# Transposing half of the row tiles on VectorE, and making low parts on GpSimd, in a low-pass MLP kernel

## What is computed

```python
# x: (16, 64, 64, 768) f32; W1: (192, 768); W2: (768, 192)
xs = einsum('bhwc,dc->bhwd', x, W1) + b1
xs = gelu(xs, approximate=False)
xs = fft_low(xs)    # 2D FFT over h, w; keep a centred 32 x 32 square of frequencies; inverse FFT; real; abs
xs = einsum('bhwd,cd->bhwc', xs, W2) + b2
return x + xs
```

## Time and profile before

| | |
|---|---|
| median of 3 runs | 2502.86 us (2502.48 to 2505.04) |
| the profiled execution | 2502.31 us, of it 2500.5 us span |
| busy: PE / DVE / ACT / POOL | 98% / 80% / 51% / 14% |
| granted PE clock | 0.995 |
| DMA | 709 MB, 284 GB/s, queue of SP 80.0% of 16 engines |

### The profile page before, as it was taken

One profiled execution on the slowest core, in us unless ns is written; L12 is line 12 of the kernel. 1 busy time (PEld: TensorE's weight loads), 2 busy tenths in 40 slices (PEclk: granted clock), 3 DMA queues, 4 the chain that ended last, 5 costly groups with the idle time before them and its releaser, 6 DMA issues.

```text
span 2500.5 us, 49622 instructions
## 1 busy us (share of the span) xinstructions
PE 2451.7 (98%) x16736; PEld 2423.6 (97%) x16736; DVE 1998.7 (80%) x4123; ACT 1272.9 (51%) x3076; POOL 350.6 (14%) x628
## 2 busy tenths in 40 slices
PE   8999999999999999999999999999999999999977
PEld 7999999999999999999999999999999999999967
DVE  6688888888888888888888888888888888888855
ACT  4555555555555555555555555555555555555532
POOL 1211111111111111111111111111111111111100
PEclk9999999999999999999999999999999999999998
DMA  6688888888888888888888888888788788878775
GB/s 201 227 281 288 291 291 292 282 299 284 295 288 293 292 285 300 286 291 291 290 293 284 299 287 290 293 288 299 280 300 290 284 292 289 296 282 299 250 281 225
DMA packets 233453, 709.29 MB, mean 284 GB/s; under 512 B 18706, under 2 KB 85522, under 8 KB 233236
## 3 DMA queue, kind: packets, MB, share of 16 engines
q1 hardware_dynamic: 233236, 706.40, 80.0%
HBM read 454.67 MB, written 251.66 MB: 282 GB/s over the span
## 4 chain that ended last, share of the span: by engine, by line
PE 95%; DMA 3%; issue 1%; DVE 1%; ACT 0%; SPq 0%; DVEq 0%; ACTq 0%
PE ps L285 23%; PE ps L272 13%; PE ps L286 11%; PE ps L331 8%; PE ps L333 7%; PE ps L332 7%; PE ps L336 7%; PE ps L339 7%; PE ps L319 5%; DMA cols<-filtered_rows 2%; PE ps L321 2%; PE ps L295 2%; PE ps L296 2%; PE ps L297 2%; DMA filtered_rows<-filt 0%
## 5 line engine op out<-in xcount | busy, mean ns | idle before, releaser
L378 ACT ACTIVATE xt_hi<-ps 128x512 fp32r<-128x512 f32 x768 | 460.1, 599 | 1121.1 <-PE ps L272 1119.0
L285 PE MATMUL ps<-w1s,xt_hi 128*128 128x384 f32 x3072 | 981.9, 375 | 0.0
L286 PE MATMUL ps<-w1s,xt_lo 128*128 128x192 f32 x3072 | 771.5, 251 | 0.0
L466 DVE TENSOR_TENSOR xt_lo<-ps,xt_hi 128x512 fp32r<-128x512 f32 x768 | 529.8, 690 | 288.3 <-ACT xt_hi L378 273.5
L518 DVE TENSOR_TENSOR xc<-ps,xc 128x384 f32<-128x384 f32 x1024 | 569.3, 556 | 135.3 <-PE ps L339 109.8
L286 PEld LDWEIGHTS ps<-w1s,xt_lo 128*128 128x128 f32 x3072 | 587.9, 191 | 0.0
L285 PEld LDWEIGHTS ps<-w1s,xt_hi 128*128 128x128 f32 x3072 | 578.9, 188 | 0.0
L272 PE MATMUL ps<-ident,xa 128*128 128x128 f32 x3072 | 462.0, 273 | 8.4 <-DMA xa<-x_dram 5.9
L272 PEld LDWEIGHTS ps<-ident,xa 128*128 128x128 f32 x3072 | 375.6, 141 | 25.5 <-issue 5.9
L331 PE MATMUL ps<-w2a_hi,oa_hi 128*128 128x384 f32 x1024 | 363.2, 355 | 0.5 <-DVE xc L518 0.5
L333 PE MATMUL ps<-w2b_lo,ob 128*128 128x384 f32 x1024 | 349.7, 341 | 0.0
(11 more groups left out here) (50 smaller groups left out, 2702.6 us busy)
## 6 DMA issues: line engine op xcount, KB each, us to landing
xa<-x_dram SPq DMA_DIRECT2D x256, 768.0 KB, 4.6
xc<-x_dram SPq DMA_DIRECT2D x256, 768.0 KB, 6.7
out_dram<-xc SPq DMA_DIRECT2D x256, 768.0 KB, 5.0
filtered_rows<-filt SPq DMA_DIRECT2D x256, 192.0 KB, 2.1
cols<-filtered_rows SPq DMA_DIRECT2D x128, 384.0 KB, 7.2
xc<-w1t_dram SPq DMA_DIRECT2D x1, 576.0 KB, 5.9
xc<-w2t_dram SPq DMA_DIRECT2D x1, 384.0 KB
xc<-w2t_dram SPq DMA_DIRECT2D x2, 192.0 KB
```

The source lines that it names most:

```text
L285: nc.tensor.matmul(ps_h[t % 2][:, 0:2 * D], hi, w1s[:, k, :], start=k == 0, stop=False)
L286: ins = nc.tensor.matmul(ps_h[t % 2][:, D:2 * D], lo, w1s[:, k, 0:D], start=False, stop=k == KC - 1)
L378: nc.scalar.activation(xt_hi[:, n % XT_SLOTS, :], ps_xt[n % 2][:], ACT.Copy).then_inc(s_xhi, 1)
L466: nc.vector.tensor_tensor(xt_lo[:, n % XT_SLOTS, :], ps_xt[n % 2][:], xt_hi[:, n % XT_SLOTS, :].bitcast(F32), ALU.subtract).then_inc(s_xlo, 1)
```

## The change

1. `xa` is split into `xv` (first tile of a pair) and `xe` (second tile). `xv` is loaded by four transfers: quarter a of the channels goes to partitions 32a to 32a + 31, pixels 32g + r to partition 32a + r and piece g. A 32x32-block transpose of DVE (`transpose_tile`) then gives the tile with channels on the partitions, in another channel order, for which `w1v` is a second, reordered copy of W1. ACT makes its high part from SBUF (`vt_hi_tile`), POOL the low part (`vt_lo_tile`).
2. The second tile is still transposed by PE, in two units of three blocks.
3. `hid_lo_pair` and `split_lo_pair` move from DVE to POOL. `split_lo_pair` runs in the turn of `filter_h_pair`, so `OUT` and the store come one turn earlier; `filter_h_pair` stands ahead of `filter_w_pair` and `out_half` in slot 0.
4. `cols` of later chunks are read a turn earlier. POOL packs at the end of its turn, and its list is written out in line, not in a loop.

```diff
-OUT = FILTER_H + 2
+OUT = FILTER_H + 1
+    x_quads = x.rearrange("b h w c -> b (h w) c").rearrange("b (t g r) c -> b t r g c", g=QUADS, r=32)
 ...
+            def load_xv(m, q):
+                until(sp, s_vt, PAIRS, m, q - X_SLOTS + 1)
+                n = q % X_SLOTS
+                for a in range(QUADS):
+                    sp.dma_start(xv[32 * a:32 * (a + 1), n, :, :],
+                                 x_quads[m, 2 * q, :, :, QC * a:QC * (a + 1)]).then_inc(s_xv[n], 16)
+            def load_xe(m, q):
+                until(sp, s_t, 2 * PAIRS, m, 2 * (q - X_SLOTS + 1))
+                n = q % X_SLOTS
+                sp.dma_start(xe[:, n, :], x_rows[m, :, 2 * q + 1, :]).then_inc(s_xe[n], 16)
 ...
-                    if (at := stage(i, s, READ_COLS)) and at[1] % 2 == 0:
-                        read_cols(at[0], at[1] // 2)
+                    if (at := stage(i, s, READ_COLS)) and (at[1] == 0 or at[1] % 2 == 1 and at[1] < PAIRS - 1):
+                        read_cols(at[0], (at[1] + 1) // 2)
 ...
 # PE
+            def transpose_unit(m, q, e):
+                if e == 0:
+                    until(pe, s_xe[q % X_SLOTS], 16 * PAIRS // X_SLOTS, m, 16 * (q // X_SLOTS + 1))
+                until(pe, s_xlo, 2 * PAIRS, m, 2 * q + e - 1)
+                for b in range(UNIT):            # UNIT = 3
+                    k = UNIT * e + b
+                    ins = nc.tensor.transpose(ps_xt[e][:, b * P:(b + 1) * P], xe[:, q % X_SLOTS, k * P:(k + 1) * P], ident[:])
+                ins.then_inc(s_t, 1)
+            def mm1_slot(m, q, j):               # four of the twelve (t, k); t 0 first
+                ...
+                    if t == 0:
+                        if k == 0:
+                            until(pe, s_vlo, PAIRS, m, q + 1)
+                        hi, lo, w1s = vt_hi[...], vt_lo[...], w1v
+                    else:
+                        if b == 0:
+                            until(pe, s_xlo, 2 * PAIRS, m, 2 * q + e + 1)
+                        hi, lo, w1s = xt_hi[...], xt_lo[...], w1e
 ...
+                            if j == 0:
+                                transpose_unit(*at, 1)
+                            if j == 2 and (after := next_pair(*at)):
+                                transpose_unit(*after, 0)
+                            mm1_slot(*at, j)
+                        if j == 0 and (at := stage(i, s, FILTER_H)):
+                            filter_h_pair(*at)
                         if j == 1 and (at := stage(i, s, LATE)):
                             filter_w_pair(*at)
 ...
                             for u in OUT_HALVES[j]:
                                 out_half(*at, u)
-                        if j == 0 and (at := stage(i, s, FILTER_H)):
-                            filter_h_pair(*at)
 ...
 # ACT, order of a turn: xt_hi_unit(pair, 1), gelu_pair(pair before), vt_hi_tile(next pair),
 #   split_hi_pair, xt_hi_unit(next pair, 0), stage_filtered
+            def vt_hi_tile(m, q):
+                until(act, s_vt, PAIRS, m, q + 1)
+                until(act, s_m1, SLOTS * PAIRS, m, SLOTS * (q - 2) + 2)
+                nc.scalar.activation(vt_hi[:, q % 2, :], vt[:, q % 2, :], ACT.Copy).then_inc(s_vhi, 1)
 ...
 # DVE, order of a turn: transpose_tile(next pair), xt_lo_unit(pair, 1), add_half; y_pair, hid_sum and
 #   hid_pre, add_half; xt_lo_unit(next pair, 0), hid_sum and hid_pre, two add_half
+            def transpose_tile(m, q):
+                until(dve, s_xv[q % X_SLOTS], 64 * PAIRS // X_SLOTS, m, 64 * (q // X_SLOTS + 1))
+                until(dve, s_vlo, PAIRS, m, q - 1)
+                nc.vector.transpose(vt[:, q % 2, :],
+                                    xv[:, q % X_SLOTS, :, :].rearrange("p g (k c) -> p k g c", c=32)).then_inc(s_vt, 1)
 ...
 # POOL, order of a turn: hid_lo_pair, corner_pair, vt_lo_tile(next pair), split_lo_pair, pack_cols_b
+            def hid_lo_pair(m, q):
+                pool.wait_ge(s_gelu, PAIRS * m + q + 1)
+                until(pool, s_f, PAIRS, m, q - 1)
+                nc.gpsimd.tensor_tensor(hid_lo[:, q % 2, :, :], hid[:, q % 2, :, :], hid_hi[:, q % 2, :, :].bitcast(F32),
+                                        ALU.subtract).then_inc(s_hlo, 1)
+            def vt_lo_tile(m, q):
+                until(pool, s_vhi, PAIRS, m, q + 1)
+                nc.gpsimd.tensor_tensor(vt_lo[:, q % 2, :], vt[:, q % 2, :], vt_hi[:, q % 2, :].bitcast(F32),
+                                        ALU.subtract).then_inc(s_vlo, 1)
+            def split_lo_pair(m, r):
+                until(pool, s_hi, PAIRS, m, r + 1)
+                yr, hi, o = y_abs[:, r % 2, :, :], oa_hi[:, r % O_SLOTS, :, :], ob[:, r % O_SLOTS, :, :]
+                nc.gpsimd.tensor_tensor(oa_lo[:, r % O_SLOTS, :, :], yr[:, 0:2, :], hi.bitcast(F32), ALU.subtract).then_inc(s_alo, 1)
+                pool.wait_ge(s_alo, PAIRS * m + r + 1)
+                nc.gpsimd.tensor_tensor(o[DB:P, 0, :], yr[0:DB, 2, :], o[0:DB, 0, :].bitcast(F32), ALU.subtract).then_inc(s_blo0, 1)
+                pool.wait_ge(s_blo0, PAIRS * m + r + 1)
+                nc.gpsimd.tensor_tensor(o[0:DB, 1, :], yr[DB:P, 2, :], o[DB:P, 1, :].bitcast(F32), ALU.subtract).then_inc(s_blo, 1)
+                pool.wait_ge(s_blo, PAIRS * m + r + 1)
```

More of the change, by code:

```diff
@@ L154, in until, with next_pair @@
                 eng.wait_ge(s, per_image * m + n)
+        def next_pair(m, q):
+            if q + 1 < PAIRS:
+                return m, q + 1
+            if whole(m) and m + 1 >= IMAGES:
+                return None
+            return m + 1, 0
         def turns(eng, turn):
@@ L523, in turn @@
                 for s in range(count):
-                    for j in range(UPP):
-                        if whole(i) and i == 0 and s == 0 and j == 0:
-                            for n in range(AHEAD):
-                                xt_lo_unit(0, n)
-                        if at := stage(i, s, 0):
-                            xt_lo_unit(at[0], UPP * at[1] + j + AHEAD)
-                        if j == 0 and (at := stage(i, s, SPLIT_LO)):
-                            split_lo_pair(*at)
-                        if j == 0 and (at := stage(i, s, LATE)):
-                            hid_lo_pair(*at)
+                    after = next_pair(*at) if (at := stage(i, s, 0)) else None
+                    for j in range(SLOTS):
+                        if i == 0 and s == 0 and j == 0:
+                            transpose_tile(0, 0)
+                            set_up_w1(w1v, w1vf, s_w1v_loaded, 64, s_w1v)
+                            xt_lo_unit(0, 0, 0)
+                            set_up_w1(w1e, w1ef, s_w1e_loaded, 16, s_w1e)
+                        if j == 0 and after:
+                            transpose_tile(*after)
+                        if j == 0 and (at := stage(i, s, 0)):
+                            xt_lo_unit(*at, 1)
+                        if j == 1 and (at := stage(i, s, FILTER_H)):
+                            y_pair(*at)
+                        if j == 2 and after:
+                            xt_lo_unit(*after, 0)
                         if j >= 1 and (at := stage(i, s, 0)):
@@ L540, in turn @@
                             corner_copy(at[0])
-                        if j == 1 and (at := stage(i, s, FILTER_H)):
-                            y_pair(*at)
                         if at := stage(i, s, OUT):
@@ L577, in turn @@
                 for s in range(count):
-                    packs = None
-                    if (at := stage(i, s, READ_COLS)) and at[1] % 2 == 0:
-                        packs = at[0], at[1] // 2
-                    if at := stage(i, s, LATE):
-                        corner_pair(*at, packs)
-                    elif packs:
-                        wait_to_pack(*packs)
-                    if packs:
-                        pack_cols_b(*packs)
-            turns(pool, turn)
+                    if i == 0 and s == 0:
+                        vt_lo_tile(0, 0)
+                    if at := stage(i, s, LATE):
+                        hid_lo_pair(*at)
+                        corner_pair(*at)
+                    if (at := stage(i, s, 0)) and (after := next_pair(*at)):
+                        vt_lo_tile(*after)
+                    if at := stage(i, s, FILTER_H):
+                        split_lo_pair(*at)
+                    if (at := stage(i, s, READ_COLS)) and at[1] % 2 == 0:
+                        pack_cols_b(at[0], at[1] // 2)
+            turns_in_line(turn)
 OUT_HALVES = [(0,), (1,), (2, 3)]
```

198 lines of the change are left out of this document (87 added, 111 removed).

## The result

The changed kernel takes 2419.4 us (median; 2412.8 to 2429.7), the kernel before 2504.0 (2502.5 to 2506.9): ratio 0.967, interval 0.9654 to 0.9685. It is faster by 84 us, where 138 were forecast; the time lies in the range, 54 us over the forecast of 2365. The profiled execution took 2429.7 us, its span is 2427.9; it is the slowest of the four, 10 us over their median, so the losses read from it are at their upper end.

A forecast was written before the change was run, and what follows sets the result against it. TensorE (PE), busy 98%, was taken as the bound, with DMA next. From 2502.3 us, 153 less for PE, +15 boundaries, +2 start, +5 image 0 and -6 tail gave 2365; 8-in-10 range 2340 to 2445 us.

The forecast's parts named there:

- PE, removed: Six of twelve transposes leave PE each turn (row pair): 0.64 us less, 9.47 to 8.83; 153 us over 239 turns.
- DVE and ACT: Per turn, DVE falls from 7.8 to 5.75 us, at most 6.7; ACT stays at 5.0; both under 8.83.
- POOL: POOL's low-part subtractions bring it to 6.1 to 7.2 us of an 8.83 us turn, leaning to 7.2: nearly full.
- Rival (c): POOL's turn passes 9.47 us if new columns cost 4.5 ns each; at 5 ns, 2700 us; chance 0.04.
- Rival (b): POOL or the wait chain comes late: `hid_lo` misses `filter_w_pair`, turn 9.0 to 9.2 us, about 2410; chance 0.12.
- none of these waits reaches PE: In the turn's layout, POOL's results come before PE asks, with about 0.9 to 2 us of slack.
- DMA: Quarter loads raise the tile from 1.03 to 1.4 to 2.15 us, the turn's DMA work to 8.1 to 8.9: just fits.
- rival (a): Transfers by quarters of the partitions become the bound: turn 9.2 us, about 2440 us in all; chance 0.18.
- Image boundary: PE stalls for `cols` of the next image by 1.0 us, range 0 to 3, at 15 images: +15 us.
- Start and image 0: A second W1 copy at the start costs +2 us; image 0 costs +5 instead of a gain of 10.
- Tail: Tail turns of about 6.4 us for 6.6, and one turn less at the end: -6 us, range -15 to +10.
- The sum: Adds all terms to the profiled 2502.3 us: 2502.3 - 153 + 15 + 2 + 5 - 6 = 2365 us.

The follow-up runs named there:

- run 7: Changed kernel with SP's loop written in line, `filter_h_pair` behind the first `out_half`, POOL's first corner sum behind `vt_lo` and later packs ahead of `split_lo_pair`: 2339.6 us.
- run 8: Changed kernel with SP's loop written in line and `hid_lo_pair` and `split_lo_pair` back on DVE, only `vt_lo` on POOL: 2371.3 us, ratio 0.9465.
- run 1: Changed kernel with SP's turns written out in line instead of a loop, nothing else: 2380.6 us, ratio 0.951.
- run 3: Changed kernel, SP's loop kept, with the first tile loaded by one transfer instead of four quarters (first product's values wrong): 2378.2 us, ratio 0.950.
- run 12: Kernel before the change with ten long-satisfied waits added to each of SP's turns and no transfer more: 2506.0 us, ratio 1.0008.
- run 9: Run 8 with `filter_h_pair` behind the first `out_half` and POOL's first corner sum of an image behind `vt_lo`: 2359.0 us, ratio 0.942.

## Why the prediction was right in sign and short in size

**PE, removed.** Right. 239 x 0.64 = 153 us were put; PE's busy time in the body is 2263.25 us before and 2112.82 in run 7, 150.4 less. The turn is 8.83 us.

**DVE and ACT.** Right. The block transpose takes 0.968 us (0.95 put), and `vt_hi` 0.84 (0.97 put). DVE's turn is 1528.7/256 = 6.0 us (5.75 put). Where the working stopped short is the question behind it: the low parts would still have fitted on DVE, and run 8 shows that they do, at 1888.9/256 = 7.4 us of DVE work in a turn of 8.83.

**POOL.** The mechanism was right, the lean too high: `vt_lo` 1.84 us and `hid_lo` 1.01 give (1.839 - 1.011)/384 = 2.16 ns a column, where 3.1 was put by the nearest row and 1.56 at the lower end; POOL is busy 61% of the span, where 70 to 80% was put. The Trainium skill's figure (GPSIMD Engine Reference, section "Performance versus the Vector engine"), from which 2.1 ns a column had been estimated, agrees with it. Rival (c) wanted 4.5 ns and is out. Rival (b), a wait in each turn, is out in mid-image. A trace of it is there once an image: POOL's first corner sum of an image waits 4.68 us for PE's `corner_sums` (L595 above) ahead of `vt_lo`, and PE waits 0.33 us for that. So "none of these waits reaches PE" held for the turn, but not for the first turn of an image, nor for the pack in the tail.

**DMA.** The quarters cost 0.36 us a tile over its 1.03 (runs 1 and 3), at the lower end of 1.4 to 2.15. The turn's DMA work is then 8.1 us, and the share 0.91 to 0.92 when PE runs undisturbed; rival (a), at 9.2 us a turn, is out. What was mis-sized is SP's side: 0.4 us were put for each of the four issues, 1.6 together, and they take 1.9 us together at the median and 2.8 or more in one case of twenty, up to 3.4. Of the halved rate at 32 partitions that the rule of the Trainium skill's page SBUF - State Buffer (section "Door 1: The DMA port swizzle") would suggest, these runs show no sign in the turn; what a single such transfer reaches alone wasn't measured.

**Image boundary.** This is the step that failed: +15 us put, 0 to 3 us a boundary as its range. It cost 69 us, or 4.6 a boundary, in two parts that the windows separate. PE idle in the body: 48.0 us, 6.8 before (2270.05 - 2263.25), so 41. PE waited for `cols` 1.90, 1.64, 4.89, 2.87, 4.05, 1.11, 3.38, 1.89, 3.90, 2.65, 2.92, 3.67, 2.52, 1.79 and 0.82 us, 40 in all; for `vt_lo` another 6.8; with some small ones these are the 48. And PE busy but slower: 2140.97 us for the work that takes 2112.82 in run 7, so 28, at a mean clock of 0.99 for 1.00. Not all of it is the clock: 9 of the 28 stand in run 1 as well (2121.59), whose granted clock is at the lower level for 7 us of the body, like that of run 7. The other 19 come with the stalls: the changed kernel's clock is at the lower level for 51 us, behind eleven of the boundaries (in runs 1 and 7 behind the first alone).

By cause, the bodies of runs 1 and 7 split the loss. Against run 7 the changed kernel's body is 70 us longer; 45 of them go with SP's loop (2188.93 - 2144.00, run 1), with the burst of quarters behind its stop, and 25 with the orders on PE and POOL (2144.00 - 2118.52). The working had a later `cols` issue in it and a fuller queue, but took SP for a row of issues that merely get longer. It didn't ask what SP does where its loop starts again. The rows of before held the sign, a stop of 0.63 us behind every sixteenth row write where 0.24 is the median, and nothing waited for it then. Nor had it a term for the clock behind a stall.

**Start and image 0**: +7 put, +3.5 measured. **Tail**: -6 put, +5 measured; the working added up the path through `y_pair`, ACT and POOL, but not POOL's pack of `cols_b`, which the change had moved behind `split_lo_pair`: seven waits of 3.0 us, 21 us in all. It is the same kind of slip: what was queued behind the moved work on its own engine.

**The sum.** By measured terms: 2502.3 - 150.4 + 69.3 + 3.5 + 5.0 = 2429.7, the profiled time; the terms are differences of the same stretches, so they add up by construction, and only their split is evidence. The two slips are 54 us at the boundaries and 11 in the tail, both to the same side; 3.5 came back at the start, and 2.6 went on PE.

## What to carry to other kernels

Before adding instructions to a queue engine that loops, look in the trace for what it does at the end of a pass, and ask which transfer stands first behind it: here a stop of 3 us was free (runs 3 and 12) or cost 39 us, by what was issued behind it. A term that comes once an image deserves its own row-by-row layout, just as the turn does; the turn was right to 0.01 us and the boundary wrong by a factor of four and a half. And moving work off an engine that isn't the bound should be priced against leaving it there, and again once the orders are right: with the low parts on DVE run 8 was 9 us faster than its twin, run 1, but run 9 19 us slower than its own, run 7.

## What the runs showed of the hardware that was not expected

SP stood still between two passes of a loop for 0.64 us with 267 recorded instructions of SP a pass, and for 3.1 to 3.4 us with 347, by ten satisfied waits more a turn; with it the packets of the instruction queue went from 82 to 145, and one started in each of the 12 stops. In line the stop is 0.04 us. That the body is fetched anew in each pass once it has passed some length fits these numbers, though the trace doesn't name the engine for which a packet was fetched. The step lies between 267 and 319 recorded instructions a pass (before, and run 3 with 2.9 to 3.1 us); no run in between was made.

Four transfers of 32 partitions with 768 B pieces kept SP for 1.9 us at the median and up to 3.4, against 0.35 for `xe`, which has the same bytes in one transfer of 128 partitions, while their cost to the DMA engines was only a third above the single transfer's.

Behind a stall of 4.9 us PE's granted clock was 0.83 over 20 us. In the body PE's slower work behind such stalls made 19 of the 69 us lost (2140.97 - 2121.59), about half as much as its added waits (41).
